# Constant bf16 products in TensorE's waits, and a new order of GpSimd's weight splits, sums and keys in the second mixture

## The reference

```
x += tanh(g_xattn[0]) * L0_xattn(ln(x), ctx)   # trilinear similarity, softmax, feats @ W_qv
x += tanh(g_ffn[0])   * L0_ffn(ln(x))          # token shift, sigmoid gate, squared relu
x += tanh(g_xattn[1]) * L1_xattn(ln(x), ctx)   # both directions of attention, interpolation, gate
x += tanh(g_ffn[1])   * L1_ffn(ln(x))          # first mixture: 8 experts, inner width 512, gelu, top 2
x += tanh(g_xattn[2]) * L2_xattn(ln(x), ctx)   # 16 heads of width 8, masked softmax
x += tanh(g_ffn[2])   * L2_ffn(ln(x))          # second mixture: 8 experts, inner 256, silu(gate)*up, grouped top 2
x += tanh(g_xattn[3]) * L3_xattn(ln(x), ctx)   # 16 heads of width 8
x += tanh(g_ffn[3])   * L3_ffn(ln(x))          # 64 tiny networks of 16 units
```

## Time and profile before

| | us |
|---|---|
| median of 3 runs | 511.95 |
| lowest, highest | 511.77, 516.05 |
| the profiled execution | 511.46 |
| its span | 509.7 |
| PE, DVE, ACT, POOL busy | 420.6, 303.1, 213.8, 123.9 |

### The profile page before, as it was taken

One profiled execution on the slowest core, in us unless ns is written; L12 is line 12 of the kernel. 1 busy time (PEld: TensorE's weight loads), 2 busy tenths in 40 slices (PEclk: granted clock), 3 DMA queues, 4 the chain that ended last, 5 costly groups with the idle time before them and its releaser, 6 DMA issues.

```text
span 509.7 us, 5546 instructions
## 1 busy us (share of the span) xinstructions
PE 420.6 (83%) x1952; PEld 337.2 (66%) x1952; DVE 303.1 (59%) x692; ACT 213.8 (42%) x391; POOL 123.9 (24%) x118
## 2 busy tenths in 40 slices
PE   3898889989999999699989686777766968997854
PEld 2675659966787888379979564555544636997744
DVE  4237780686677777875552657644353479765064
ACT  2103222256879897254331424423143324553153
POOL 4001182120435262203040401122242222000052
PEclk9999755559999999999886858877597887997559
DMA  6500001000541312001000000141230000000001
GB/s 203 207 2 0 1 0 41 1 1 6 163 145 42 124 57 69 0 1 40 24 1 1 0 0 6 39 144 61 74 91 24 21 0 2 0 1 1 0 0 41
DMA packets 13343, 20.85 MB, mean 41 GB/s; under 512 B 1787, under 2 KB 5397, under 8 KB 13317
## 3 DMA queue, kind: packets, MB, share of 16 engines
q1 hardware_dynamic: 12768, 20.03, 12.3%
q0 software_dynamic: 96, 0.32, 0.2%
q10 hardware_dynamic: 453, 0.18, 0.1%
HBM read 19.92 MB, written 0.59 MB: 40 GB/s over the span
## 4 chain that ended last, share of the span: by engine, by line
PE 56%; DVE 20%; issue 10%; ACT 6%; POOL 5%; DMA 1%; ACTq 0%; DVEq 0%; POOLq 0%
PE bank L1370 9%; PE bank L1371 8%; PE bank L1372 8%; PE bank L1691 7%; PE bank L1673 3%; PE bank L1378 2%; POOL wb L466 2%; PE bank L1405 2%; DVE Sx L1234 2%; DVE small L1233 2%; DVE h L868 2%; DVE stats L856 2%; DVE x L1031 1%; DMA ctxN<-in_ctx 1%; DVE rlo L1176 1%
## 5 line engine op out<-in xcount | busy, mean ns | idle before, releaser
L1370 PE MATMUL bank<-hhi,wuh 128*128 128x512 f32 x128 | 59.5, 465 | 14.3 <-POOL wul L449 13.8
L1370 PE MATMUL bank<-rhi,wdh 128*128 128x512 f32 x96 | 42.7, 445 | 23.1 <-DVE rlo L1293 11.0
L424 POOL TENSOR_TENSOR rstd<-var,neghalf 128x4 f32<-128x4 f32 x16 | 16.7, 1042 | 176.6 <-DVE var L861 176.6
L1284 DVE TENSOR_TENSOR bank<-shared,bank 128x512 f32<-128x512 f32 x32 | 22.2, 695 | 62.2 <-PE bank L1372 55.9
L1176 DVE TENSOR_TENSOR rlo<-bank,rhi 128x512 fp32r<-128x512 f32 x64 | 44.1, 691 | 23.3 <-ACT rhi L706 22.6
L1371 PE MATMUL bank<-hlo,wuh 128*128 128x512 f32 x128 | 56.5, 441 | 0.0
L1372 PE MATMUL bank<-hhi,wul 128*128 128x512 f32 x128 | 56.2, 439 | 0.0
L722 ACT ACTIVATE bank<-bank,b1s 128x512 f32<-128x512 f32 x64 | 42.3, 660 | 18.2 <-PE bank L1372 17.9
L1691 PEld LDWEIGHTS bank<-vals,shared 128*128 128x128 f32 x320 | 45.6, 226 | 5.8 <-issue 5.3
L1691 PE MATMUL bank<-vals,shared 128*128 128x27 f32 (+1 forms) x320 | 45.7, 300 | 4.0 <-DVE wa L1245 4.0
L793 ACT ACTIVATE shared<-bank 128x512 f32<-128x512 f32 x32 | 19.0, 597 | 68.5 <-PE bank L1372 68.5
(11 more groups left out here) (279 smaller groups left out, 875.1 us busy)
## 6 DMA issues: line engine op xcount, KB each, us to landing
rowB<-rowd SPq DMA_DIRECT2D x32, 256.0 KB, 3.4
up_raw<-in_w SPq DMA_DIRECT2D x8, 258.0 KB, 4.5
down_raw<-in_w SPq DMA_DIRECT2D x8, 256.0 KB, 4.9
up_raw<-in_v SPq DMA_DIRECT2D x8, 256.0 KB, 3.3
down_raw<-in_v SPq DMA_DIRECT2D x8, 128.0 KB, 3.8
const<-in_const SPq DMA_DIRECT2D x1, 911.0 KB, 7.2
mats<-in_mats SPq DMA_DIRECT2D x1, 640.0 KB, 5.3
mats<-in_mats SPq DMA_DIRECT2D x1, 576.0 KB, 4.1
```

Source lines behind the costliest of these rows:

```text
L1284: V.tensor_tensor(bank[BANKU[g % 3]][:, :], silu[g % 2], bank[BANKU[g % 3]][:, :], ALU.mult).then_inc(r["mul"], 1)
L1370: mm(o, lh, rh, start=start, stop=False)
```

## The change

A bf16 tile `heat` of ones is filled by POOL at the start. `keep_busy(bank, n)` on PE multiplies it with itself n times into a bank that holds nothing at that moment; its result is never read. 51 such calls, 194 products of 128x512 in all, are placed ahead of waits: in every layer but inside the loops of the mixtures (there only at g = 0 and 1 of the second) and inside the units of the attentions. In the second mixture POOL's order is new: in pass i it splits both experts' up weights and the first's down weights for pass i + 1, and the four keys of the last attention, which had been made at the start of the mixture, follow in the passes. ACT makes the high parts to match. The first batch's routing on DVE is moved ahead, into the attention's end, and PE's `router(1, 0, 10)` ahead of the last `values_of`.

```diff
+            nc.gpsimd.memset(heat[:, :], 1.0).then_inc(heat_ready, 1)
             nc.gpsimd.memset(neghalf[:, :], -0.5)
...
             for b in range(B):
                 mask_values(1, b)
+            for b in range(B):
+                norm(10 + b)
             pool.wait_ge(kv["hi"], 2)
-            for b in range(B):
-                norm(10 + b)
-                if b == 0:
-                    pool.wait_ge(at["S"], 3 * NT * B)
-                for half in range(2):
-                    key(b, half)
+            pool.wait_ge(at["S"], 3 * NT * B)
 
             split_up(1, 0, r)
+            split_up(1, 1, r)
+            split_down(1, 0, C2, r)
             for i in range(1, PASSES):
-                split_up(i, 1, r)
-                split_down(i, 0, C2, r)
+                split_down(i, 1, C2, r)
                 if i == 1:
                     add(1, "r", r)
                 else:
                     add(4 * i - 1, "r", r)
-                split_down(i, 1, C2, r)
+                if i > 1:
+                    key(i - 2, 1)
                 add(4 * i, "r", r)
+                if i < LAST:
+                    key(i - 1, 0)
+                    split_up(i + 1, 0, r)
                 add(4 * i + 1, "r", r)
-                if i == LAST:
+                if i < LAST:
+                    split_up(i + 1, 1, r)
+                    split_down(i + 1, 0, C2, r)
+                else:
                     norm(12)
-                if i < LAST:
-                    split_up(i + 1, 0, r)
                 if i == 1:
                     add(3, "r", r)
                 add(4 * i + 2, "r", r)
...
-                if n == 0 and i > 0:
-                    up_hi(i, 1, 1, N2, r, r["u"])
                 if n == 1 and i > 0:
-                    down_hi(i, 0, N2, C2, r)
-                if n == 3 and i > 0:
                     down_hi(i, 1, N2, C2, r)
-                if n == 6 and i < LAST:
+                if n == 5 and i < LAST:
                     up_hi(i + 1, 0, 1, N2, r, r["u"])
+                if n == 7 and i < LAST:
+                    up_hi(i + 1, 1, 1, N2, r, r["u"])
+                    down_hi(i + 1, 0, N2, C2, r)
...
-                if g in (4, 7):
-                    routing_tanh(1, (g - 4) // 3)
+                if g in (0, 7):
+                    routing_tanh(1, g // 7)
...
                 if n == 0:
                     parts(10, 0)
+                    logits(1, 0)
+                    best_groups(0)
                 normalise(NT * B - 1)
                 return attended
 
             attended = attend(0)
-            logits(1, 0)
+            compare(0, ex, E, lt8)
+            argument(1, 0)
...
+            def keep_busy(o, n):
+
+                for _ in range(n):
+                    mm(o[:, :], heat[:, 0:P], heat[:, :], start=True, stop=True)
+
...
+            pe.wait_ge(heat_ready, 1)
+            keep_busy(bank[3], 14)
             pe.wait_ge(ld["ident"], 16)
...
+            keep_busy(bank[6], 8)
             transposes(6)
+            keep_busy(bank[5], 3)
             router(0, 0, 6)
+            keep_busy(bank[5], 5)
...
                 pe.wait_ge(nb_ready, 1)
+                keep_busy(bank[5], 4)
                 transposes(base)
+                keep_busy(bank[5], 3)
                 queries(0)
...
                 transposes(base + 2)
+                if n == 0:
+                    router(1, 0, 10)
+                keep_busy(bank[1], 6)
                 values_of(NT * B - 1)
...
-            router(1, 0, 10)
             pe.wait_ge(m["split"], 3)
             pe.wait_ge(at["sub"], 3 * NT * B)
             hidden2(0)
+            keep_busy(bank[2], 4)
...
+                if g < 2:
+                    keep_busy(bank[7], 8)
                 down(g, C2, "r", r)
...
+            keep_busy(bank[5], 14)
             transposes(15)
+            keep_busy(bank[5], 3)
             hidden_of(1)
...
             for b in range(B):
+                keep_busy(bank[5], 4 + 6 * b)
                 ffn_out(b)
```

More of the change, by code:

```diff
@@ L137, in flamingo_program @@
         ident_b = sb("ident_b", [P, P], BF16)
+        heat = sb("heat", [P, S], BF16)
         tg = sb("tg", [P, 8])
@@ L224, in flamingo_program @@
         dve_step, pool_step = sem("dve_step"), sem("pool_step")
-        ready_const = sem("ready_const")
+        ready_const, heat_ready = sem("ready_const"), sem("heat_ready")
         ln_var, ln_rstd, ln_h, ln_T, hT_ready = [sem(n) for n in ("ln_var", "ln_rstd", "ln_h", "ln_T", "hT_ready")]
@@ L516, in _ @@
                 mask_values(1, b)
-            pool.wait_ge(kv["hi"], 2)
             for b in range(B):
                 norm(10 + b)
-                if b == 0:
-                    pool.wait_ge(at["S"], 3 * NT * B)
-                for half in range(2):
-                    key(b, half)
+            pool.wait_ge(kv["hi"], 2)
+            pool.wait_ge(at["S"], 3 * NT * B)
             split_up(1, 0, r)
+            split_up(1, 1, r)
+            split_down(1, 0, C2, r)
             for i in range(1, PASSES):
-                split_up(i, 1, r)
-                split_down(i, 0, C2, r)
+                split_down(i, 1, C2, r)
                 if i == 1:
@@ L1301, in _ @@
                 if g == 1:
-                    best_groups(0)
+                    weights(1, 0)
                 if g == 3:
-                    compare(0, ex, E, lt8)
-                    argument(1, 0)
-                if g == 4:
-                    weights(1, 0)
                     logits(1, 1)
+                    best_groups(1)
                 if g == 5:
-                    best_groups(1)
+                    compare(1, ex, E, lt8)
                 if g == 6:
-                    compare(1, ex, E, lt8)
                     argument(1, 1)
@@ L1418, in _ @@
             last.then_inc(p0_pe, 1)
+            keep_busy(bank[3], 3)
             transposes(1)
@@ L1435, in token_max_everywhere @@
                    start=True, stop=True).then_inc(l0["mB"], 1)
-            for b in range(B):
-                token_max(b)
-                token_max_everywhere(b)
+            keep_busy(bank[7], 4)
+            token_max(0)
+            keep_busy(bank[7], 2)
+            token_max_everywhere(0)
+            keep_busy(bank[7], 2)
+            token_max(1)
+            keep_busy(bank[2], 2)
+            token_max_everywhere(1)
+            keep_busy(bank[2], 3)
             def probabilities_T(b):
@@ L1465, in _ @@
             probabilities_T(0)
+            keep_busy(bank[3], 2)
             attended(0)
+            keep_busy(bank[6], 2)
             probabilities_T(1)
+            keep_busy(bank[1], 2)
             output(0)
+            keep_busy(bank[7], 2)
             attended(1)
+            keep_busy(bank[5], 2)
             output(1)
+            keep_busy(bank[0], 4)
             transposes(2)
@@ L1519, in _ @@
             replicate(0, 0)
+            keep_busy(bank[0], 5)
             for b in range(B):
                 transposes(4 + b)
+                keep_busy(bank[4 * b + 2], 2)
                 pe.wait_ge(kv["reps"], 1)
@@ L1528, in _ @@
             for b in range(B):
+                keep_busy(bank[4 * b], 3)
                 pe.wait_ge(l2["exp2"], b + 1)
@@ L1544, in _ @@
             for b in range(B):
+                keep_busy(bank[4 * b + 1], 2)
                 pe.wait_ge(l2["PTs"], b + 1)
@@ L1554, in _ @@
             for b in range(B):
+                keep_busy(bank[4 * b + 3], 2)
                 pe.wait_ge(l2["s2cs"], b + 1)
```

## The result

The changed kernel takes 468.74 us (median of 466.28, 468.33, 469.15 and 485.82), the kernel before on the same chip 511.86. The ratio is 0.914, with an interval of 0.905 to 0.923: faster by 8.6%. The execution at 485.82 ran at a mean clock of 0.807, the others at 0.920 to 0.927, and is left out of the ratio. The prediction was 444, its range 428 to 474: the sign and the range held, the forecast was 25 us too low, and the time lies outside the forecast's own range of 430 to 458.

A forecast was written before the change was run, and what follows sets the result against it. TensorE was taken as bound by its 1.2 GHz clock in several stretches and by waits in the second mixture. Terms summed to -67.8 from 511.5, giving 444 us; own range 430 to 458, 8-in-10 range 428 to 474.

The forecast's parts named there:

- The passes from step 4: Second mixture from step 4: splits made a pass earlier remove TensorE's waits and the clock stays high, 68.4 against 113.0, -44.6.
- new waits for `rlo`: Sign of being wrong: in the second mixture's passes TensorE would newly wait some us a pass for `rlo`.
- The entry: X update to step 4 of the second mixture: keys and first batch's routing gone from there, -5.3 (-3 to -7).
- The keys beside DVE's passes: Keys moved into the second mixture's passes: DVE's operations there read PSUM and are not slowed, nothing charged.
- The first layer: From 8.7 to 34.6: TensorE's busy time halves at the high clock, less the constant products' cost, -7.8 (-4 to -10).
- The L1 attention and the entry to the first mixture: From 58.8 to 116.5: dense work from 75.7 on gets the high clock, -9.0 (range -13 to +4).
- Rival 1: Clock rises only where real work is dense, so short groups of constant products pay: 470 us, chance 0.17.
- The third attention: Four products at its start cost +0.9; its end, with twelve, open between -2 and +5, taken as +2.
- The last attention's head: Ahead of the last attention, where waits are longer and a stretch of 14.2 ran at 0.64: -2 (-3 to 0).
- The end: From 464.6 on: TensorE's products halve behind fourteen constant products in a wait, -2, bounds -5 and +3.
- rival 2: Second mixture's passes: keys and sums on POOL keep the first split late, the clock falls with it; 474 us, chance 0.10.
- The clock that does not follow (3): Rival: constant products do not raise the clock, all 194 cost 0.43, the kernel gets slower: 520 us, chance 0.04.

The follow-up runs named there:

- e1: The changed kernel with all 194 constant products left out, the new order alone: 473.14 us against 511.12 for the kernel before, ratio 0.930.
- e7: e5 with the second batch's `best_groups` on VectorE moved one step later, from g = 3 to g = 4: 453.66 us, ratio 0.899.
- e5: e4 with the fifth expert's weight load issued ahead of the two row loads of the second mixture's first pass: 463.38 us.
- e9: e7 with the fifth expert's load moved ahead of the store of the second batch's weights, where SyncE's queue is empty: 458.59 us, ratio 0.902.
- e3: The changed kernel with the last attention's four keys back between the norms at the second mixture's entry: 469.22 us.
- e8: e4 without the 16 constant products at g < 2 of the second mixture's entry: 461.88 us against e4's 461.43.
- e2: The kernel before with all 194 constant products in place and none of the new order: 498.31 us, ratio 0.977.
- e6: `heat` filled with zeros in place of ones; no execution time is given.
- e10: e9 with the second mixture's router for the first batch, and its routing on VectorE, behind the last values again: 455.79 us.
- e11: e10 with the twelve constant products around the third attention's end put back: 459.31 us.
- e4: The changed kernel without the twelve constant products around the third attention's end, the router still ahead: 461.43 us, ratio 0.902.
- a2: The changed kernel measured again, unchanged, on the chip of e9 and e10: 466.49 us against 510.00 for the kernel before, ratio 0.920.

## Why the prediction was right or wrong

**The passes from step 4** were forecast at -44.6 and gave 113.0 less 78.0, and by the same marks (step 4 to the last `down`, 112.1 before) -34.1. This is the term that was mis-sized most, by 10. The mechanism was right: the splits' waits went from 21.5 to 1.2, less than the 3.0 allowed, and e1 shows that it is the order alone. Where the 78.0 go, counted in the changed kernel's products: 59.3 of work as forecast, 12.0 in fifteen waits of over 0.2 (forecast 7.8), 3.9 for twenty products at 0.43 instead of 0.23 (forecast 0), 2.1 in short handovers; the rest are the transposes among them (forecast 1.3 for both). So 4.2 us more of waits and the clock's falls, 3.9, are most of what the sum left out. Two points of the prediction failed here:
- "since in pass 0 the second batch's routing still stands on DVE between two subtractions: 4 of the 5.5." It was not followed into the new order, in which it stands in one piece at g = 3 (before, `logits` at 4 and `best_groups` at 5), meets POOL's split, and the clock falls behind it. Parted, steps 4 to 8 take 2.7 less (e7).
- SyncE's queue was not followed at all. The new order and the shorter steps want the fifth expert's weights sooner, and they were issued behind four row loads: 3.1 on ScalarE. e5 and e9 show the cause. Ahead of the row loads the load brings nothing (e5), in an empty queue 1.8 (e9).

The first split's own wait was priced rightly: 1.5 twice was forecast, and it is 1.2 ahead of step 24 and, ahead of step 16, hidden by the wait for `rlo` here and 1.6 in e7 and e9. "That dense passes hold the high level" was right between the waits, but behind each of the three longest (2.8, 1.8, 1.2) it fell to 0.50 for 3.4 us. Of the signs that the prediction gave of being wrong, "new waits for `rlo`" of some us a pass came: 4.2 in pass 1.

**The entry**, forecast -5.3, gave -2.8 (14.6 to 11.8). The keys were charged the whole 3.4 of the norm; e3 finds 1.7 on the path. The sixteen products were charged 0.9 and cost 0.2 (e8). The 1.9 for the routing is not there: e2 and e3 differ by 0.1.

**The keys beside DVE's passes** were rightly taken as free: e3 has no gain of over 1 us from taking them away. The operations of 128x512 that read PSUM kept their 0.68 to 0.69 beside the keys in the passes too. In another place, one that had not been looked at, meeting POOL did decide: routing operations on VectorE with both inputs in SBUF took 1.27 and 1.10 instead of some 0.2, each ending within 0.1 of POOL's split. What the prediction took from the Trainium skill, the row on the shared port pair, is the short form. The same page of the Trainium skill (SBUF — State Buffer, Who interferes with whom) says that a VectorE instruction with at most one SBUF input, outside its 2-port modes, does not contend with GpSimd, and one with two does, against a GpSimd instruction that reads SBUF. By that rule 0.69 and 1.27 are both as they should be: the trace agrees.

**The first layer**, forecast -7.8, gave -5.9 in the profiled execution and -5.4 to -7.7 over all twelve traces with products; -0.8 without (e1). Where the clock did not fall at 14 to 18, as it did in the changed kernel, it is -6.7 to -7.7, near the size forecast.

**The L1 attention and the entry to the first mixture**, forecast -9.0, gave -4.0 from the first x update to step 16 of the first mixture (98.5 to 94.5). In seven other traces, e2, e5, e6, e7, e9, e10 and e11, it is 91.3 to 91.4, which is some -7.2: the size hangs on where the clock falls. The clock was low at 68.8 to 75.6, as said, and at 89.2 to 92.6 and 99.5 to 106.3, which was not. Rival 1, that it stays low there, is out.

**The third attention.** At its start +0.75 (forecast +0.9), of which 0.3 is left by the first scores. Its end, forecast +2, bound +5, gave +5.9: 4.2 from `transposes(10)` on, 1.7 in `values_of(6)` ahead. The bound was for the products alone. What failed is that router and products were priced apart: each by itself costs less than 1 (e10: 0.9; e11: -0.7), together 4.2 and in three more traces 4.7 to 5.5. With the router ahead, its wait of 0.7 for the copied h comes first, and router, products, values and `hidden2(0)` all run at 0.50; that this wait is what brings the low clock is argued from the order of the traces and not shown. The 1.7 in `values_of(6)` is the clock's place in this execution: e6 and e11, with the same products, don't have it.

**The last attention's head**, forecast -2, gave +0.3; in e4, e6, e7 and a2 it gave -1.0. **The end**, forecast -2, gave -5.0, the good bound, and that is partly luck. From the last attention's first x update to the last x update it takes 46.2 before and 44.1 in e1, without products. Of the twelve traces with products six have 41.0 to 41.4 (the changed kernel, a2, e6, e7, e9, e10) and six 45.0 to 45.4 (e2, e3, e4, e5, e8, e11), though all have the same products there. So the products at the end are worth 3 or cost 1 against e1, by where the clock falls.

**The rivals.** The wait that takes the place of the one removed did come, not at the split, where rival 2 had it, but at DVE's routing and in SyncE's queue. The clock that does not follow (3) is out by e2. e2 is 12.8 us faster, a ratio of 0.977, with 194 products more to do. The Trainium skill (TensorE: Matmul & The Clock Gate, What's actually happening) says that for modeling the ramp penalty is under 1% of a typical span, and it tells this of a kernel's start. Here the start alone disagrees: products in the first layer give 5.4 to 7.7 us of 509.7, over 1%, and 174.7 us of the span before are at 0.50 besides.

Two slips in the prediction's figures change nothing: 258 x 0.23/0.80 + 9 is 83.2 and not 83.6, and 34.6 + 58 + 34 is just under a quarter of the span. That the time came within the range rests in part on the end, which gave 3 more than forecast in this trace and gave 1 less than forecast in six others.

**A better version** is among e7, e9 and e10: 453.7 to 458.6, where the changed kernel has 466.5 to 468.7, and a2 ran on the chip of e9 and e10. Which of the three is best, these runs don't tell.

## What to carry to other kernels

When work moves ahead, or the steps in front of it get shorter, follow what it reads back to the queue that loads it: the transfer's place in that queue may have to move too, into a gap, since ahead of another transfer it only passes the wait on. Price a filler product together with whatever stands around it: the same twelve gave 0.7 right behind dense work, and cost about 4 behind the router and its wait. And take the order first: where it removed the waits, the clock was 0.93 with no filler in the loop. A stretch in which the clock falls at other places from execution to execution needs several traces before a gain in it is believed.

## What the runs showed of the hardware

- Constant products raise the granted clock, with zeros as with ones: the first layer ran at 1.00 and ended at 29.9 with zeros, at 29.7 to 32.0 with ones, at 36.6 with none (first x updates of e6, of the other traces with products, of e1).
- Where the clock falls moves from execution to execution, and it decides some us each time: the same end of the program took 41.0 to 41.4 in six traces and 45.0 to 45.4 in six others. The changed kernel spent 68.3 us of its span at 0.50, e7 44.6, e1 135.9, besides the time ahead of the record's start (34.2 in e1).
- A short VectorE operation with its inputs in SBUF that starts beside a GpSimd split ends with it: 128x32 in 1.27 instead of 0.19. Operations of 128x512 that read PSUM kept 0.68 to 0.69 beside keys of 2.3.
